# Attention of an eight-head block with MoE: the second and third product issued per key tile, and one map normalised at a time

## What is computed

```
q1, q2, k1, k2 = each RMS-normalised over its 128 channels
y1 = causal_softmax(q1 k1^T / sqrt(128)) v
y2 = causal_softmax(q2 k2^T / sqrt(128)) v
y  = y1 - lambda * y2
x1 = layernorm(x + (y wo^T) * 0.2)
```

## Time and profile before

| | us |
|---|---|
| median of the timed runs | 9834.32 |
| the three timed runs | 9647.31, 9834.32, 10132.6 |
| the profiled execution's own time | 9169.97 |
| its span, slowest core (core 4) | 9168.4 |
| spans of the eight cores | 9072.5 to 9168.4 |
| granted TensorE clock, mean over the span | 0.884 to 0.889 |

### The profile page before, as it was taken

The page is one execution under the profiler, slowest core; times in us unless marked ns, Lnnn a source line. Parts: engine busy times, 40 slices in busy tenths (PEclk is TensorE's granted clock), DMA queues, the critical chain, the costliest instruction groups (busy, mean ns, idle before and its releaser), DMA issues.

```text
span 9168.4 us, 80319 instructions; the slowest of 8 cores (9072.5 to 9168.4 us)
## 1 busy us (share of the span) xinstructions
PE 7327.3 (80%) x32866; PEld 3250.6 (35%) x32866; DVE 1962.1 (21%) x2644; ACT 2474.4 (27%) x2841; POOL 924.3 (10%) x822
## 2 busy tenths in 40 slices
PE   4545646645648459999999999997999999999996
PEld 2222222212213124444444444433444444444442
DVE  1222222222221521111111111123111111111113
ACT  3665675675571020101101101111010010010011
POOL 0000000000000001111111111111111111111110
PEclk8767767767767779999999999998999999999998
DMA  4001001001003137877777777865777777777684
GB/s 61 5 10 14 5 10 14 7 8 14 10 5 78 32 29 71 79 67 71 76 69 72 76 69 71 76 61 84 70 70 76 70 72 75 73 70 74 67 81 69
DMA packets 1663577, 483.64 MB, mean 53 GB/s; under 512 B 1589097, under 2 KB 1655017, under 8 KB 1661170
## 3 DMA queue, kind: packets, MB, share of 16 engines
q0 software_dynamic: 1655712, 444.71, 49.4%
q1 hardware_dynamic: 7506, 33.80, 1.0%
HBM read 906.34 MB, written 16.78 MB: 101 GB/s over the span
## 4 chain that ended last, share of the span: by engine, by line
PE 68%; ACT 12%; DMA 7%; issue 7%; DVE 5%; another core or an unknown queue 1%; DVEq 0%; POOL 0%; ACTq 0%; SPq 0%; POOLq 0%
PE PB L985 15%; PE PB L916 10%; PE PB L922 9%; PE P L916 9%; PE P L922 9%; DMA WOS<-wom 6%; PE PB L284 4%; ACT ATT L481 4%; ACT L481 3%; PE PB L499 3%; PE PB L594 3%; ACT L374 2%; PE P L493 2%; PE PB L318 1%; DMA WI1S<-wi 1%
## 5 line engine op out<-in xcount | busy, mean ns | idle before, releaser
L985 PE MATMUL PB<-H,WOS 128*128 128x512 bf16 x8192 | 1846.5, 386 | 198.8 <-DMA WOS<-wom 100.8
L938 ACT ACT_TABLE_LOAD x256 | 328.4, 1283 | 4824.1 <-PE PB L922 3355.9
L985 PEld LDWEIGHTS PB<-H,WOS 128*128 128x128 bf16 x8192 | 800.0, 99 | 1245.4 <-issue 354.0
L436 PE MATMUL PB<-QT,KT 128*128 128x512 bf16 (+3 forms) x640 | 295.8, 480 | 809.9 <-ACT ATT L481 809.9
L481 ACT ACT_TABLE_LOAD x640 | 821.1, 1283 | 345.9 <-PE PB L436 216.7
L916 PE MATMUL PB<-X1T,WI0S 128*128 128x512 bf16 x4096 | 910.1, 381 | 3.7 <-DMA WI1S<-wi 3.4
L916 PE MATMUL P<-X1T,WI0S 128*128 128x512 bf16 x4096 | 904.9, 379 | 3.6 <-DMA WI1S<-wi 3.6
L922 PE MATMUL PB<-X1T,WI1S 128*128 128x512 bf16 x4096 | 904.9, 379 | 0.0
L922 PE MATMUL P<-X1T,WI1S 128*128 128x512 bf16 x4096 | 904.9, 379 | 0.0
L902 POOL DMA_DIRECT2D WI0S<-wi x256 | 293.1, 1145 | 3245.1 <-PE PB L922 1897.2
L1000 DVE TENSOR_TENSOR ACC<-ACC,PB 128x512 f32<-128x512 f32 x448 | 307.9, 687 | 1415.4 <-PE PB L985 1415.4
(11 more groups left out here) (120 smaller groups left out, 4619.5 us busy)
## 6 DMA issues: line engine op xcount, KB each, us to landing
WI0S<-wi POOLq DMA_DIRECT2D x256, 512.0 KB, 6.5
WI1S<-wi POOLq DMA_DIRECT2D x256, 512.0 KB, 8.6
WOS<-wom POOLq DMA_DIRECT2D x256, 512.0 KB, 6.4
OXF<-xt SPq DMA_DIRECT2D x16, 1024.0 KB, 6.4
outT<-OUTS SPq DMA_DIRECT2D x32, 512.0 KB, 2.6
XT<-xt POOLq DMA_DIRECT2D x16, 512.0 KB, 28.6
WS<-wqT POOLq DMA_DIRECT2D x8, 1024.0 KB, 12.1
WS<-wkT POOLq DMA_DIRECT2D x8, 1024.0 KB, 11.7
```

The lines of the kernel that those rows point to most:

```text
L436: _t.out = PT.inc(t.matmul(PB[bn][:, qs:512], KT[:, m * T + kt * 128: m * T + (kt + 1) * 128], QT[:, m * T + qb * 512 + qs: m * T + (qb + ...
L938: i = PS.inc(s.activation(SILU[:, c * 512:(c + 1) * 512], h0p[par][c][1], AF.Silu))
L985: mm = t.matmul(PB[bn][:], WOS[slot][:, mt * 128:(mt + 1) * 128], H[:, mt * TCH + c * 512: mt * TCH + (c + 1) * 512], start=(mt == 0), sto ...
```

## The change

Three edits in the function that builds the program:

```diff
-            k1n_by_m = [0, 0]
             for m in range(2):
                 for side in range(2):
...
                         k1n_val = _v.out
-                        k1n_by_m[m] = _v.out
                     sq_cons[0] = mmv
 
-            for m in range(2):
-                k1n_val = k1n_by_m[m]
...
-                    def _t(t, qb=qb, nkt=nkt, exp_done=exp_done):
-                        wait_banks(t, ["P2a", "PB2", "PB3"])
-                        for kt in range(nkt):
-                            qs = max(0, kt * 128 - qb * 512)
+                        def _tda(t, kt=kt, qb=qb, qs=qs, nkt=nkt):
+                            if kt == 0:
+                                wait_banks(t, ["P2a", "PB2", "PB3"])
                             wt(t, "t", (PS, exp_done[kt]))
                             t.matmul(P2[:, qs:512], ONESB[:],
                                      ATT[:, kt * 512 + qs: (kt + 1) * 512],
                                      start=(kt == 0), stop=(kt == nkt - 1))
-                        for ct in range(2):
-                            for kt in range(nkt):
-                                qs = max(0, kt * 128 - qb * 512)
+                            for ct in range(2):
                                 mm = t.matmul(PB[2 + ct][:, qs:512],
                                               VTOK[:, kt * HD + ct * 128: kt * HD + (ct + 1) * 128],
                                               ATT[:, kt * 512 + qs: (kt + 1) * 512],
                                               start=(kt == 0), stop=(kt == nkt - 1))
-                        _t.out = PT.inc(mm)
-                    TS(_t)
-                    av_val = _t.out
-                    for kt in range(nkt):
-                        att_cons[kt] = (PT, av_val)
+                            _tda.out = PT.inc(mm)
+                        TS(_tda)
+                        att_cons[kt] = (PT, _tda.out)
+                        av_val = _tda.out
...
-        x1_jt = [None] * TT
...
-            x1_jt[jt] = (PV, _v.out)
...
     def _t(t):
+        wt(t, "t", x1_done)
         wt(t, "t", (LDG, ld_xt))
         wait_banks(t, p2_dep_all)
         for dt in range(DT):
-            if x1_jt[dt] is not None:
-                wt(t, "t", x1_jt[dt])
```

## The result

The changed kernel is slower, by a ratio of 1.1238 with a 95% interval from 1.1124 to 1.1351. Over ten runs each the medians are 10513.94 us (10251.8 to 11140.49) against 9751.01 us (9155.53 to 10384.96), 763 us apart.

What follows compares the result with a forecast made beforehand. ScalarE was taken to bound the score phase, TensorE the product phase. Per head 308.6 + 20.1 + 54.6 + 5.0 = 388.3 us instead of 251.9, so 1091 us over eight heads, added to the median: about 10920 us, range 10250 to 11250.

Steps and rivals of the forecast that it cites:

- The closed chain: Attention, per key tile: next scores stand behind products awaiting the exponential; full step 4.02 us, 308.6 us per head.
- The clock: Attention: TensorE's short bursts with waits between keep it at 1.2 GHz, PEclk near 0.50; all four matmuls priced so.
- The reading that pauses of 2.3 us are harmless: Attention: only a pause beyond a certain length takes TensorE's full clock away; would give +634 us.
- Rival 1: Attention: TensorE's clock stays at 2.4 GHz; +634 us, 10470 us; chance 0.06.
- The bank waits: Query block borders: first products wait for the previous block's scaling, 2.4 and 4.3 us excess; 20.1 us per head.
- The moved normalisation: Between the maps: map 1's normalisation waits on VectorE behind map 0's last scaling; 5.0 us per head.
- The edits at nothing: Gate logits' wait, exponential's finer wait on ATT, GpSimd's weight loads and added TensorE blocks: 0 us.
- The 576 additional blocks: TensorE's added blocks: 0 us, since matmuls overlap across a branch; upper bound 192 us over 640 steps.
- The sum: All heads: 388.3 us per head instead of 251.9, 1091 us more over eight; 10261 us on the profiled execution's time.
- rival 2: Key tile: next scores pass waiting products, ScalarE stays the bound at 1.91 us; -336 us, 9500 us; chance 0.03.
- From the profile to the median: Whole kernel: timed median lay 665 us above the profiled execution; 1091 us added to that median, about 10920 us.
- rival 4: Whole kernel: the gap between profiled and timed runs goes away, median 10260 us; chance 0.14.

Runs made afterwards that it cites:

- e7: Changed kernel with one activation table load per query block instead of per key tile; heads stretch (head 0's first squaring to first output-projection matmul) 2988 us.
- e6: Changed kernel with both maps normalised first and each key tile's products queued behind the next tile's score matmul; heads stretch 2533 us.
- e10: Changed kernel with nine wasted matmuls per key tile ahead of the bank wait, 22 where a block waits for the one before; heads stretch 3328.9 us.
- e5: Changed kernel with a second set of output banks for odd query blocks; heads stretch 3551 us.
- e2: Kernel before with only map 1's normalisation moved between the attention of map 0 and of map 1; heads stretch 2661.2 us.
- e1: Kernel before with only the gate logits waiting for x1_done first instead of slice by slice; heads stretch 2636.3 us.
- e4: Changed kernel with nine wasted matmuls ahead of each key tile's products, behind the bank wait; heads stretch 3493.5 us.

## Why the prediction was right

The time lies in the stated range, and the loss came by the chain that was named. Step by step:

- **The closed chain.** "So two banks buy nothing any more": the step was to be 4.02 us and is 3.98. A map's attention, from its first score matmul to the end of its last products, was 154.3 us of steps and 7.2 of bank waits, 161.5 us; it is 160.7 (184.25 to 345.0). For map 1 the same sum, with 12.9 us of bank waits, gives 167.2 us, and it is 166.3 (377.27 to 543.56). That the chain is the cause, and not the interleaving as such, is shown from both sides: one link shortened by 1.28 us shortens the step by as much (e7), and opening the chain at the place named makes the same product groups faster than the batch before (e6).
- **The clock.** 0.50 in both attentions, as forecast. The section "Loop structure matters more than you think" of the page "TensorE: Matmul & The Clock Gate" of the Trainium skill, which I had weighed, speaks of a long wait for a transfer ahead of every matmul; the trace agrees with its direction, with waits of 2.12 us ahead of every burst of four matmuls, and of 0.84 us in e7. The reading that pauses of 2.3 us are harmless does not hold. TensorE comes out of the normalisation at 0.50 and never leaves it in after or in e7. I wrote that no run showed this yet, but the kernel before did. On its core 4, behind the product phase of query block 1, the granted clock is 1.00 from 243 to 245 us, 0.59 from 245 to 247 and 0.50 from then on, with single score matmuls and no wait longer than 2.18 us:

```profile
243.97 0.38 PE L436 MATMUL PB<-QT,KT 128*128 128x512 bf16 x1 [2.18 <-ACT ATT L481]
245.88 0.58 PE L436 MATMUL PB<-QT,KT 128*128 128x512 bf16 x1 [1.53 <-ACT ATT L481]
```

  Rival 1's price was near: +634 us were worked out for 2.4 GHz, and e10, whose attention is held there, has +692.
- **The bank waits.** 20.1 us per head forecast, 21.2 by e5.
- **The moved normalisation.** Here the reasoning was wrong and the number was not. I wrote that the scaling of map 0's last block "before lay beside map 1's first scores". It did not: masks and scaling are both on VectorE, in order, and the first exponential waited for both [e2]. The sum did not suffer, since a head's time after was added up from its parts and subtracted from a measured time of before. As the price of this edit, the 5.0 us per head are 3.1 us alone and 2.0 us in company.
- **The edits at nothing.** The gate's wait is worth 0 (e1). The 576 additional blocks cost nothing that can be seen: the sum without them is already 1.7 us per head too high (388.3 against 386.6).
- **The sum.** 1091 us forecast, 1084.5 measured in the heads stretch. For head 0 it was 136.4 us forecast and 134.7 measured. Eight times 134.7 are 1078; the stretch grew by more because the other heads had been up to 0.8 us shorter than head 0 before. On the profiled execution's time this gave 10261 us; the fastest execution of after took 10251.8 us. The ratio of 1.119 lies in the measured interval. Two small slips change nothing: 410.6 to 417.33 us are 6.7 us and not 6.8, and the chances of "faster" and "same" add up to 0.04, though rival 2 has 0.03.
- **From the profile to the median.** The step that was off is "so I add the 1091 us to the median": 10920 us against 10513.94. Three runs were a poor basis for the median of before: they took 9647 to 10133 us, while of the ten of before three took less than 9300. By the medians the change costs 763 us and not 1091. I had kept this apart as rival 4 and gave it 0.14; its 10260 us are where the fastest execution lies, and the measured median is between it and the forecast. That the median lies in the range is owed to the range's width, which takes in rivals 4 and 1; it does not confirm the 665 us that were added.

Rival 2, that scores pass waiting products, did not happen: there is no tile at 1.91 us in after. What it would have been worth is what e6 does by hand.

## What to carry to other kernels

Before interleaving two stages in one in-order queue, draw the cycle: if what stands next in the queue is needed by the engine whose result the queue is waiting for, the double buffer is dead and the step is the sum of both engines' shares, at whatever clock the pauses leave. Put the consumer one tile behind the next producer, never between a producer and its successor; the same three matmuls per tile then cost nothing in a full tile (1.91 us a step, e6) instead of 2 us. In a chain like this every link counts in full, so look at the cheap ones too: a table load per tile was a third of the step.

## What was not expected of the hardware

Wasted work made the kernel faster. 5760 matmuls of 512 columns that nobody reads took 227 us off the heads stretch (e4), and 6384 of them, ahead of the bank wait, took 392 us off (e10): they fill pauses that TensorE would otherwise spend idle, and the granted clock of the attention goes from 0.50 to 0.93 and 0.99. It is no way to build a kernel, since e6 needs none of it and is 796 us below e10, but it is a way to measure what the clock costs.

The output projection, an unbroken run of matmuls, is not always at the full clock either: in the profile of before it took 409.0 us to the gate on cores 4 to 7, with a granted clock of 0.87 from 2795 to 3046 us on core 4, and 381.8 us on core 0, with 0.99. What sets that was not tried.
